# Heads' projection of a decoder layer: two fp32 products per head, or six single-pass products of high and low parts

## The reference, cut to what matters

```
q, k, v = x @ Wq, x @ Wk, x @ Wv          # per head: 256 x 128 each
q, k = rmsnorm(q), rmsnorm(k)
attn = softmax(causal(q k^T / sqrt(128) + alibi))
y = rmsnorm(attn @ v) * subln_w           # 256 x 128 per head
x = layernorm(x + concat(y) @ Wproj)      # Wproj: 2048 x 256
x = layernorm(x + x @ softmax(...))       # cross attention with ctx
x = layernorm(x + bitlinear feed-forward(x))
```

## Time and profile before

| | before |
|---|---|
| median of 3 runs | 432.35 us (432.35 to 432.9) |
| the profiled execution | 433.11 us |
| its span, first to last instruction | 431.3 us |
| TensorE matmul, weight loads busy | 400.9 us, 368.1 us |
| VectorE, ScalarE, GpSimd busy | 298.5 us, 281.4 us, 181.0 us |
| mean granted TensorE clock, share of full | 0.971 |

### The profile page before, as it was taken

One profiled execution on the slowest core, in us unless ns is written; L12 is line 12 of the kernel. 1 busy time (PEld: TensorE's weight loads), 2 busy tenths in 40 slices (PEclk: granted clock), 3 DMA queues, 4 the chain that ended last, 5 costly groups with the idle time before them and its releaser, 6 DMA issues.

```text
span 431.3 us, 8778 instructions
## 1 busy us (share of the span) xinstructions
PE 400.9 (93%) x2610; PEld 368.1 (85%) x2620; DVE 298.5 (69%) x933; ACT 281.4 (65%) x800; POOL 181.0 (42%) x283
## 2 busy tenths in 40 slices
PE   4699999999999999999999999999999999997653
PEld 3599998999999998999999998999999999986421
DVE  4678878876777577767576576667575676675695
ACT  3287876677777587667857587667757577764251
POOL 3676766633334333335435333335344343322301
PEclk9699999999999999999999999999999999999885
DMA  7999200000000000000002000000000000000000
GB/s 192 276 296 325 71 1 2 2 0 15 0 26 2 2 2 2 0 2 0 2 2 61 2 0 3 0 2 2 1 2 26 0 2 1 2 2 2 1 24 24
DMA packets 21662, 14.84 MB, mean 34 GB/s; under 512 B 1648, under 2 KB 21360, under 8 KB 21616
## 3 DMA queue, kind: packets, MB, share of 16 engines
q1 hardware_dynamic: 20800, 13.90, 11.1%
q10 hardware_dynamic: 816, 0.39, 0.3%
HBM read 13.24 MB, written 1.05 MB: 33 GB/s over the span
## 4 chain that ended last, share of the span: by engine, by line
PE 87%; DVE 7%; issue 2%; POOL 1%; DMA 1%; ACT 1%; POOLq 0%; DVEq 0%; ACTq 0%
PE ps L504 31%; PE ps L546 12%; PE ps L514 7%; PE ps L527 7%; PE ps L521 5%; PE ps L526 3%; PE ps L533 3%; PE ps L535 3%; PE ps L534 3%; PE ps L554 3%; PE ps L467 2%; PE ps L455 1%; DMA x_sb<-in_x 1%; PE ps L477 1%; PE ps L416 1%
## 5 line engine op out<-in xcount | busy, mean ns | idle before, releaser
L376 POOL TENSOR_TENSOR qk_rstd<-qk_sum,minus_half 128x2 f32<-128x2 f32 x128 | 92.8, 725 | 115.3 <-DVE qk_sum L829 114.7
L504 PE MATMUL ps<-w_hi,xT_hi 128*128 128x384 f32 x256 | 101.7, 399 | 4.1 <-DVE qk_n L823 2.3
L829 DVE TENSOR_REDUCE qk_sum<-sq 128x2 f32<-128x258 f32 x128 | 53.9, 421 | 74.2 <-ACT sq L709 70.2
L709 ACT ACTIVATE sq<-ps 128x256 f32<-128x256 f32 x128 | 49.3, 386 | 74.2 <-PE ps L504 74.1
L504 PE MATMUL ps<-w_hi,xT_lo 128*128 128x384 f32 x256 | 87.2, 342 | 0.0
L371 POOL TENSOR_TENSOR y_rstd<-y_sum,minus_half 128x2 f32<-128x2 f32 x64 | 47.3, 740 | 94.8 <-DVE y_sum L1067 93.2
L504 PE MATMUL ps<-w_lo,xT_hi 128*128 128x384 f32 x256 | 86.9, 341 | 0.0
L823 DVE TENSOR_TENSOR qk_n<-ps,qk_rstd 128x256 f32<-128x256 f32 x128 | 53.9, 421 | 33.4 <-POOL qk_rstd L376 33.2
L546 PE MATMUL ps<-wp,yT 128*128 128x256 f32 x256 | 66.0, 380 | 1.1 <-ACT yT L737 1.1
L504 PEld LDWEIGHTS ps<-w_hi,xT_hi 128*128 128x128 f32 x256 | 49.3, 193 | 8.0 <-issue 2.5
L504 PEld LDWEIGHTS ps<-w_lo,xT_hi 128*128 128x128 f32 x256 | 49.2, 193 | 1.3 <-POOL w_lo L331 0.3
(11 more groups left out here) (184 smaller groups left out, 780.1 us busy)
## 6 DMA issues: line engine op xcount, KB each, us to landing
wp<-in_L_attn_Wproj SPq DMA_DIRECT2D x4, 512.0 KB, 5.9
x_sb<-in_x SPq DMA_DIRECT2D x4, 256.0 KB, 3.4
ff_raw<-in_L_ffn_w_gate SPq DMA_DIRECT2D x1, 1024.0 KB, 7.9
ff_raw<-in_L_ffn_w_up SPq DMA_DIRECT2D x1, 1024.0 KB, 10.4
w_raw<-in_L_attn_Wq SPq DMA_DIRECT2D x4, 256.0 KB, 7.1
w_raw<-in_L_attn_Wk SPq DMA_DIRECT2D x4, 256.0 KB, 5.7
w_raw<-in_L_attn_Wv SPq DMA_DIRECT2D x4, 256.0 KB, 5.6
ff_raw<-in_L_ffn_w_down SPq DMA_DIRECT2D x1, 1024.0 KB, 8.1
```

What stands on the lines that cost most here:

```text
L376: pool.tensor_tensor(qk_rstd[:, t, :], qk_sum[:, t, :], minus_half[:], ALU.pow).then_inc(s_rs[t], 1)
L504: last = pe.matmul(ps[:, t, 0:W3], xa[:, b % 2, k, tok], wa[:, h, k * W3:(k + 1) * W3], start=(i == 0), stop=(i == len(parts) - 1))
L709: act.activation(sq[:, t, :, 0:D], ps[:, t, 0:2 * D].rearrange("p (a d) -> p a d", a=2), ACT.Square).then_inc(s_sq[t], 1)
L829: dve.tensor_reduce(qk_sum[:, t, :], sq[:, t], AX.X, ALU.add).then_inc(s_ss[t], 1)
```

## The change: what it does

`Wproj` and `yT` get high and low parts as x and the qkv weights have. ScalarE makes `wp_hi` by a copy to fp32r, one head in each of steps 3 to 18; GpSimd subtracts to make `wp_lo` in the same steps. ScalarE's scaled copy of yT now writes fp32r (`yT_hi`), and VectorE computes `yT_lo` from the same PSUM tile by a scalar_tensor_tensor, in every step, between `y_sum` (with the splits behind it) and `sums(n, 0)`. `project` issues three fp32r products for each 128 tokens instead of one fp32 product, and waits for `yT_lo`.

To make room, `prob` shares the memory of `score`, `v_sb` has three buffers instead of four, `attn` one instead of two, the cross projections lie in `attn_raw`, `hq` lies in a part of `ff_raw` that x1 also uses (x1 and x2 trade places), and the absolute values go to `attn`. Some waits are moved for that.

```diff
-        wp = sb("wp", [P, H, C])
-        yT = sb("yT", [P, 2, T])
+        wp_hi = sb("wp_hi", [P, H, C], F32R)
+        with nc.sbuf_tensor("wp_raw", [P, H, C], F32) as wp_raw:
+            pass
+        wp_lo = sb("wp_lo", [P, H, C], F32R)
+        yT_hi = sb("yT_hi", [P, 2, T], F32R)
+        yT_lo = sb("yT_lo", [P, 2, T], F32R)
...
-        prob = sb("prob", [P, 3 * P])
+        prob = score
...
-        v_sb = sb("v_sb", [P, 4, TT, VW])
+        v_sb = sb("v_sb", [P, 3, TT, VW])
...
+        qcT, kcT = attn_raw[:, 0], attn_raw[:, 1]
+        attn = sb("attn", [P, TT, T])
...
+        hq = ff_raw[:, 0, 1024:2048].bitcast(BF16).rearrange("p (t f) -> p t f", t=TT)
+        abs_w = attn[:].rearrange("p k t -> p (k t)").bitcast(BF16)
...
@@ gpsimd, step n, after tile 1's rstd and split_lo
+                        if t == 1 and 0 <= n - 3 < H:
+                            h = n - 3
+                            pool.wait_ge(s_wphi, h + 1)
+                            pool.tensor_tensor(wp_lo[:, h], wp_raw[:, h], wp_hi[:, h].bitcast(F32),
+                                               ALU.subtract).then_inc(s_wplo, 1)
...
@@ tensor, project(n)
-                pe.wait_ge(s_yT, n + 1)
+                pe.wait_ge(s_yTlo, n + 1)
...
-                if b == 0 and h % 4 == 0:
-                    pe.wait_ge(s_wp[h // 4], 16)
+                if b == 0:
+                    pe.wait_ge(s_wplo, h + 1)
                 for t in range(TT):
-                    last = pe.matmul(total[:, t * C:(t + 1) * C], yT[:, n % 2, t * P:(t + 1) * P], wp[:, h, :],
-                                     start=(h == 0 and t == 0), stop=(h == H - 1), skip_group_check=True)
+                    for i, (ya, wa) in enumerate(((yT_hi, wp_hi), (yT_hi, wp_lo), (yT_lo, wp_hi))):
+                        last = pe.matmul(total[:, t * C:(t + 1) * C], ya[:, n % 2, t * P:(t + 1) * P], wa[:, h, :],
+                                         start=(h == 0 and t == 0 and i == 0), stop=(h == H - 1 and i == 2),
+                                         skip_group_check=True)
...
@@ tensor, turn_y(n)
-                wait(pe, s_yT, n)
+                wait(pe, s_yTlo, n)
...
@@ scalar, squares(n, 0)
-                    wait(act, s_y, n - 3)
+                    wait(act, s_y, n - 2)
...
@@ scalar, step n
-                    wait(act, s_tp, m)
...
-                    act.activation(yT[:, m % 2, :], ps_yT, ACT.Copy, scale=sub_scale).then_inc(s_yT, 1)
+                    act.activation(yT_hi[:, m % 2, :], ps_yT, ACT.Copy, scale=sub_scale).then_inc(s_yT, 1)
...
+                if 0 <= n - 3 < H:
+                    h = n - 3
+                    if h % 4 == 0:
+                        act.wait_ge(s_wp[h // 4], 16)
+                    act.copy(wp_hi[:, h], wp_raw[:, h]).then_inc(s_wphi, 1)
...
@@ vector, norm_x1
+                if b == LAST:
+                    dve.wait_ge(s_th2, 1)
+                elif b > 0:
+                    dve.wait_ge(s_side_in, JOB["hq_turn", b - 1, 1] + 1)
...
@@ vector, step n, ahead of sums(n, 0)
+                if 0 <= n - 4 < STEPS:
+                    m = n - 4
+                    dve.wait_ge(s_yT, m + 1)
+                    dve.scalar_tensor_tensor(out=yT_lo[:, m % 2], in0=ps_yT, scalar=sub_scale,
+                                             in1=yT_hi[:, m % 2].bitcast(F32), op0=ALU.mult,
+                                             op1=ALU.subtract).then_inc(s_yTlo, 1)
...
@@ vector, biased scores
-                    wait(dve, s_p, m)
+                    wait(dve, s_tp, m)
```

More of the change, by code:

```diff
@@ L126, in decoder_kernel @@
         ctxT = sb("ctxT", [P, T])
-        qcT = sb("qcT", [P, T])
-        kcT = sb("kcT", [P, T])
         attn_raw = sb("attn_raw", [P, TT, T])
-        attn = sb("attn", [P, 2, TT, T])
+        qcT, kcT = attn_raw[:, 0], attn_raw[:, 1]
+        attn = sb("attn", [P, TT, T])
         neg_xmax = sb("neg_xmax", [P, TT])
@@ L146, in decoder_kernel @@
         res = ff_raw[:, 0, 0:TT * C].rearrange("p (t c) -> p t c", t=TT)
-        x1 = ff_raw[:, 0, 512:1024].rearrange("p (t c) -> p t c", t=TT)
-        x2 = ff_raw[:, 0, 1024:1536].rearrange("p (t c) -> p t c", t=TT)
+        x2 = ff_raw[:, 0, 512:1024].rearrange("p (t c) -> p t c", t=TT)
+        x1 = ff_raw[:, 0, 1024:1536].rearrange("p (t c) -> p t c", t=TT)
         x1T = ff_raw[:, 0, 1536:2048].rearrange("p (k t) -> p k t", k=KC)
@@ L154, in decoder_kernel @@
         hT = ff_raw[:, 2, 1024:2048].bitcast(BF16).rearrange("p (t f q) -> p t f q", t=TT, f=FC)
-        hq = sb("hq", [P, TT, F], BF16)
-        abs_w = hq[:, 0]
+        hq = ff_raw[:, 0, 1024:2048].bitcast(BF16).rearrange("p (t f) -> p t f", t=TT)
+        abs_w = attn[:].rearrange("p k t -> p (k t)").bitcast(BF16)
         stats = sb("stats", [P, TT, nc.vector.BN_STATS_DIM])
@@ L184, in decoder_kernel @@
             "constants_set", "w_hi_set", "w_lo_set", "dist_set", "vecs_scaled"))
+        s_wphi, s_wplo, s_yTlo = sem("wp_hi_set"), sem("wp_lo_set"), sem("yT_lo_set")
         s_w0hi, s_w1hi = sem("w_head0_hi_set"), sem("w_head1_hi_set")
@@ L264, in load_wp @@
             def load_wp(i):
-                sp.dma_start(wp[:, 4 * i:4 * i + 4, :], wp_d[:, 4 * i:4 * i + 4, :]).then_inc(s_wp[i], 16)
+                sp.dma_start(wp_raw[:, 4 * i:4 * i + 4, :], wp_d[:, 4 * i:4 * i + 4, :]).then_inc(s_wp[i], 16)
             load_x(0)
@@ L455, in slot @@
                             last = pe.matmul(side[:, t * T:(t + 1) * T], x1T[:, k, t * P:(t + 1) * P],
-                                             attn[:, b % 2, k, :], start=(k == 0), stop=(k == TT - 1))
+                                             attn[:, k, :], start=(k == 0), stop=(k == TT - 1))
                 elif kind == "xq_turn":
@@ L531, in values @@
                 wait(pe, s_yn, n)
-                v = v_sb[:, n % 4]
+                v = v_sb[:, n % 3]
                 pe.matmul(ps_y[:, 0, :], pT[:, 0:P], v[:, 0, :], start=True, stop=True)
@@ L606, in _ @@
                 for k in range(TT):
-                    last = pe.matmul(ps[:, 4 * t + 1, 0:T], x1T[:, k, t * P:(t + 1) * P], attn[:, LAST % 2, k, :],
+                    last = pe.matmul(ps[:, 4 * t + 1, 0:T], x1T[:, k, t * P:(t + 1) * P], attn[:, k, :],
                                      start=(k == 0), stop=(k == TT - 1))
@@ L675, in side_read @@
                     act.wait_ge(s_side_in, turned)
-                    act.copy(attn[:, b % 2].rearrange("p k t -> p (k t)"), side).then_inc(s_side_out, 1)
+                    act.copy(attn[:].rearrange("p k t -> p (k t)"), side).then_inc(s_side_out, 1)
                 elif kind == "x_turn":
@@ L711, in squares @@
                 if t == 0:
-                    wait(act, s_y, n - 3)
-                act.copy(v_sb[:, n % 4, t, 0:D], ps[:, t, 2 * D:3 * D]).then_inc(s_v[t], 1)
+                    wait(act, s_y, n - 2)
+                act.copy(v_sb[:, n % 3, t, 0:D], ps[:, t, 2 * D:3 * D]).then_inc(s_v[t], 1)
             for a in range(3):
```

## The result

The changed kernel took 434.53 us (median of 15 executions, 432.66 to 435.59) against 432.9 us (15 executions, 431.84 to 433.46): a ratio of 1.0036, 95% interval 1.0025 to 1.0047. It is slower by 0.36%, a little, and the interval excludes no change. The forecast was 428.0 us, 424.8 to 431.2; sign and range both missed. The profiled execution has a span of 432.7 us, 1.4 more than before.

A forecast was written before the change was run, and what follows sets the result against it. It took TensorE's work in program order to set the end in the middle of the kernel. Products -7.8, VectorE's early steps +1.7 and the tail +1.7 gave -4.4 us: 432.35 to 428.0 us, range 424.8 to 431.2.

The forecast's parts named there:

- Edits costed at nothing: ScalarE's wp_hi copies, GpSimd's 16 subtractions of 0.77 us, transfers and memory sharing with moved waits: all priced at zero.
- VectorE's extra instruction: yT_lo on VectorE: 0.39 us a step, hidden from step 13 on, costing 1.7 us in steps 4 to 12.
- The six products: Projection on TensorE: 0.116 us each, 0.70 us for 0.87, 0.17 us saved a step, 7.8 us counting in all.
- The 0.121: Alternative cost in us of one projection product, with a fixed 0.014 us paid whatever its width; it gave 428.9 us.
- the rival of the narrow product: Projection products of 256 columns cost 0.174 us like the wide ones; 442 to 443 us, slower; chance 0.09.
- products that are not three: Without single passes each projection product costs 0.217 us, the projection 1.3 us; 21 us slower; chance 0.01.
- The tail: At the end, yT_lo(63) queues behind VectorE's quantising; the projection result is taken 1.7 us later, bounds 1.2 and 2.1.
- VectorE becomes the bound: yT_lo unhidden in all 27 steps with gaps up to 0.43 us; 436 us, slower or same; chance 0.12.
- All of it counts: Early steps and tail cost nothing and a projection product takes 0.109 us; 423 us; chance 0.06.
- the price of zero for the memory: Shared buffers cost nothing, since each moved wait is on a TensorE job earlier in its order or many steps back.

The follow-up runs named there:

- wplo_moved: Changed kernel with GpSimd's wp_lo of heads 9 to 15 made one step later, behind tile 0's qk_rstd; 431.24 us, 0.9979 of the kernel before.
- no_wplo: Changed kernel without GpSimd's subtraction, second product reading wp_hi, yT_lo still made (timing only); 429.54 us, 0.9929 of the kernel before.
- all_three: Changed kernel with later wp_lo from head 9, last yT_lo between the quantising halves, yT_lo behind sums(n, 0); 427.85 us, 0.9895 of the kernel before.
- products: Changed kernel without yT_lo and wp_lo, six products reading high parts only (timing only); 426.53 us, 0.9848 of the kernel before.
- share: Kernel before with only the changed kernel's memory sharing and moved waits, projection in fp32 as before; 432.88 us, 0.9996 of the kernel before.
- no_ytlo: Changed kernel without VectorE's yT_lo, third product reading yT_hi again, wp_lo still made (timing only); 429.09 us, 0.9917 of the kernel before.
- hybrid: Changed kernel with batch 0 projected in fp32, Wproj parts made in steps 16 to 32, last yT_lo between quantising halves; 429.68 us, 0.9934 of the kernel before.
- tail: Changed kernel with the last yT_lo(63) made between the two tiles quantised in step 66; 432.26 us, 0.9992 of the kernel before.
- behind_sums: Changed kernel with yT_lo moved behind sums(n, 0) in VectorE's order; 432.18 us, 0.9987 of the kernel before.

## Why the prediction was wrong, by its own steps

Its sum, cut at the same places, was about -0.3 us up to `turn_qk(18)`, -5.8 to `turn_qk(63)` and +1.7 for the tail, -4.4 together. Measured in the profiles: +3.01, -4.70, and +2.57 with +0.48 behind the take; +1.4 together. Of the 5.8 us between them, 3.3 lie in the first part, 1.1 in the middle, 1.4 at the end.

**"Edits costed at nothing" is the step that failed.** It priced GpSimd's 16 subtractions by the engine's own idle time, found it waiting for VectorE, and put down zero, or at most 0.4 us in nine steps if `y_rstd` came late. Nothing came late on GpSimd. The subtraction lengthened what VectorE was doing at that moment, from SBUF to SBUF, ahead of `norm(n, 1)`. The cost is 2.71 us with `wp_lo` as the only low part and 88.15 - 84.44 = 3.71 beside `yT_lo`; 2.02 of the 3.71 go when those of heads 9 to 15 alone are moved. The other 1.69 is the difference between `wplo_moved` and `no_wplo`, and by their starts of `turn_qk` it lies in steps 7, 10 and 12 alone, 0.56, 0.55 and 0.57 us. Each of the three has a VectorE instruction lengthened beside `wp_lo` in `wplo_moved`: a cast of 1.11 us (at 47.70), a quantising instruction of 0.83 (at 70.61), a cast of 1.12 (at 77.71). That is read from the traces; no run moved these. In `all_three`, where `yT_lo` no longer takes the room, the subtractions left in their place cost 84.14 - 83.39 = 0.75 us. The trace of before held the sign. Timelines of GpSimd and of VectorE in its step 12:

```profile
80.25 0.81 POOL L326 TENSOR_TENSOR w_lo<-w_raw,w_hi 128x256 fp32r<-128x256 f32 x1
...
80.50 0.84 DVE L1025 TENSOR_SCALAR ff_raw<-ff_raw 128x512 f32<-128x512 f32 x1
81.38 0.43 DVE L1029 TENSOR_SCALAR ff_q<-ff_raw 128x512 bf16<-128x512 f32 x1
```

The quantising instruction took 0.84 us beside a piece of `w_lo`, and the next one of that kind, with GpSimd done, 0.43. I read the mean of a group (462 ns) and not its long members.

The Trainium skill has the rule, in "SBUF — State Buffer", section Who interferes with whom: VectorE and GpSimd share a port pair as an exclusive lock, and a `cast` or `tensor_scalar` of VectorE can take both of its ports, so that whichever engine comes second is blocked until the other has finished. The runs agree that the second one is lengthened: 0.84 us for L1047 beside `wp_lo`, 0.43 without. At 88.53 `wp_lo` had 0.56 us to go and 0.41 were added, so that all of the rest is waited for isn't shown. By that page a VectorE instruction with at most one input in SBUF and outside these modes doesn't contend, which is why `wp_lo` beside norms out of PSUM and sums could be expected to be free. `wplo_moved` agrees: up to 130 us, 29 of its norms run beside a subtraction, and each takes 0.41 to 0.43 us, as the others do.

**VectorE's extra instruction** was sized right: 0.478 us, hidden from step 13 on (18 to 63 is 265.74 us with it and 265.58 without), and 1.7 us forecast for the steps up to 12 against 1.05 measured with no `wp_lo` beside it. What the step missed is that the two low parts together cost 1.00 us more than the sum of each alone: both lengthen the same round of VectorE, and once the room of a step is used up, the second counts in full. Step 12 became 6.94 us where it was 5.58; `turn_qk` waits in 26 steps instead of 11.

**The six products** were under-priced by a little: 0.72 us for 0.70, so 0.15 us a step for 0.17. The 0.121 that the text worked out beside the 0.116, with a fixed part for each product, was the right one of the two. With it the middle would have been put at about -5 us; measured are -4.70, and -4.90 in `products`. By this the rival of the narrow product falls, which needed 0.132 us, and with it that of products that are not three.

**The tail** was right in its mechanism and short in size. `yT_lo(63)` stood behind the quantising as described, and ended 1.6 us earlier than forecast because the whole end lay earlier; the order cost 1.91 us for 1.7. Not foreseen was the 0.66 us of slower products. The 0.48 us behind the take have no cause on record: among the 13 profiles that stretch takes 32.25 to 33.20 us, 33.09 in `products`, whose last products kept their pace, and 32.42 in `share`, and 6 us behind the take the profiles are up to 0.97 us apart already.

**The rivals.** *VectorE becomes the bound* gave the nearest time, 436, for a reason that is only partly its own: it has TensorE held back by VectorE in all steps with little room, and time was lost so in the early steps alone. From 18 to 63 nothing of it is seen, as `no_ytlo` has the same time there as the changed kernel. *All of it counts* fails by the same stage table. That `share` is the same in all of these stages confirms the price of zero for the memory; the reasons given for it weren't tried one by one.

So of the loss 0.48 us stay without a cause. Uncertain too is how much of it the clock takes: see the last section.

## What to carry to other kernels

Work put into an idle engine is free only if the instruction that runs beside it, on another engine, isn't lengthened by it, and if nothing waits for that engine's next reply (step 32 of `hybrid`): for a new GpSimd instruction, look at what VectorE does in that very stretch, and look at the longest and shortest member of its groups rather than the mean. An instruction added to a full round belongs behind the one that sends work away, not ahead of it, so that it fills the wait for the answer. A gain of 4.70 us spread over 45 steps was undone by 3.07 in fifteen others and 3.05 at the end, so cut the span into stages before adding up.

## What was not expected of the hardware

Beside a GpSimd subtraction of 128x256, VectorE's `tensor_scalar` on 128x512 took 0.84 us for 0.43, and its cast on 128x768 1.10 us (at 47.38, with `wp_lo` from 47.34) for 0.55. GpSimd's own `wp_lo` ranged from 0.74 to 0.92 us.

The granted clock fell at the end. Windows of the changed kernel (us; busy TensorE, weight loads, VectorE, ScalarE, GpSimd; granted clock; DMA share, GB/s), then those of `tail` in a fence of its own:

```profile
392.00:400.00 8.00, 4.61 (x32) 4.04 (x31) 4.83 (x10) 1.34 (x3) 0.69 (x1) 0.82 0.01 2
400.00:408.00 8.00, 6.77 (x32) 5.05 (x30) 4.52 (x14) 2.67 (x4) 2.38 (x6) 0.54 0.00 0
```

```profile
392.00:400.00 8.00, 4.02 (x36) 3.02 (x35) 6.65 (x15) 2.87 (x4) 2.13 (x5) 1.00 0.01 2
400.00:408.00 8.00, 5.89 (x29) 4.28 (x28) 5.33 (x19) 0.74 (x2) 1.81 (x5) 0.79 0.00 0
```

After 2.31 us without work TensorE went at the lower of its two levels (0.54 is close to 1.2 of 2.4 GHz), and products 0.12 us apart became 0.21 apart; after 1.08 us in `tail` it stayed at 1.00 up to 400; the 0.79 behind that the kernel before has too, from 398.60 to 406.60. `wplo_moved` and `behind_sums` fell as the changed kernel did, but `no_wplo`, with the same 2.31 us wait, kept 0.12 us products. So in the 13 profiles the products slowed only behind that wait, and not each time. Over the 15 executions of the changed kernel the five with a mean granted clock of 0.977 or more have spans of 430.9 to 432.1 us, the ten with 0.971 or less 432.1 to 433.3. What decides between them no run here shows.
